# A two-layer decoder on one NeuronCore: the fourth convolution tile ahead of the state-space scan moves from TensorE to ScalarE and VectorE

## The reference

```
xn = x * rsqrt(mean(x * x, -1) + EPS) * norm_w            # x is already layer-normalised
x_inner, z = split(einsum('bld,ed->ble', xn, in_proj_w))  # 512 channels each
xc = conv1d(x_inner, conv_w, causal, 4 taps, one filter per channel) + conv_b
xc = silu(xc)
x_ssm = einsum('bld,ed->ble', xc, x_proj_w)               # 16 B, 16 C, 1 dt for each token
dt = softplus(x_ssm[..., -1:] * dt_w[:, 0] + dt_b)        # 512 channels
h  = exp(dt * A) * h + (dt * xc) * B ;  y = sum(h * C) + D_param * xc      # the scan, 128 steps
out = (y * silu(z)) @ out_proj_w + x
```

## Time and profile before

| | |
|---|---|
| median of 3 runs | 904.55 us (903.81 to 906.38) |
| the profiled execution | 906.09 us, its span 904.3 us |
| busy: PE, PEld | 732.1 us (81%), 525.2 us (58%) |
| busy: DVE | 718.4 us (79%) |
| busy: ACT | 541.4 us (60%) |
| busy: POOL | 521.5 us (58%) |
| mean granted TensorE clock | 0.898 |

### The profile page before, as it was taken

One profiled execution on the slowest core, in us unless ns is written; L12 is line 12 of the kernel. 1 busy time (PEld: TensorE's weight loads), 2 busy tenths in 40 slices (PEclk: granted clock), 3 DMA queues, 4 the chain that ended last, 5 costly groups with the idle time before them and its releaser, 6 DMA issues. The chain is left out here.

```text
span 904.3 us, 14551 instructions
## 1 busy us (share of the span) xinstructions
PE 732.1 (81%) x4298; PEld 525.2 (58%) x4301; DVE 718.4 (79%) x1533; ACT 541.4 (60%) x1377; POOL 521.5 (58%) x542
## 2 busy tenths in 40 slices
PE   5899999999999884499999149959999999940365
PEld 3578888888888762377777124345555555630232
DVE  6667788888898875677777578497999999679886
ACT  2545565555556552466666525778998788037195
POOL 2057777777777861355553576627888799422211
PEclk8899999999999997599999559969999999975586
DMA  8726000000000500365546230032223222100000
GB/s 315 226 85 289 1 2 1 8 1 7 8 1 8 200 7 12 122 226 147 147 143 124 75 100 29 4 117 70 93 93 100 87 94 93 37 10 0 0 18 30
DMA packets 29932, 70.80 MB, mean 78 GB/s; under 512 B 5440, under 2 KB 19584, under 8 KB 27552
## 3 DMA queue, kind: packets, MB, share of 16 engines
q1 hardware_dynamic: 25248, 57.28, 17.5%
q0 software_dynamic: 4608, 12.59, 5.6%
HBM read 59.30 MB, written 10.55 MB: 77 GB/s over the span
## 5 line engine op out<-in xcount | busy, mean ns | idle before, releaser
L1857 POOL TENSOR_TENSOR arena<-arena 128x1024 f32<-128x1024 f32 x63 | 148.4, 2382 | 45.7 <-DVE arena L1779 45.7
L1779 DVE TENSOR_TENSOR_SCAN arena<-arena,ps 128x1024 f32<-128x1024 f32 x64 | 143.7, 2277 | 12.6 <-PE ps L1504 7.3
L1525 PE MATMUL ps<-arena 128*128 128x512 f32 x256 | 120.1, 592 | 0.0
L645 PE MATMUL ps<-arena 128*128 128x128 f32 (+1 forms) x768 | 101.1, 282 | 0.9 <-PEq L373 0.9
L1086 POOL DMA_INDIRECT arena<-tokens,arena x64 | 62.6, 979 | 67.4 <-PE ps L1114 50.5
L645 PEld LDWEIGHTS ps<-arena 128*128 128x128 f32 (+1 forms) x768 | 91.6, 193 | 14.1 <-issue 12.9
L850 ACT ACTIVATE arena<-arena 128x128 f32<-128x128 f32 x256 | 98.8, 389 | 1.2 <-DVE arena L774 1.1
L858 ACT ACTIVATE arena<-ps 128x512 f32<-128x512 f32 x64 | 38.2, 597 | 86.6 <-PE ps L664 86.6
L1652 ACT ACTIVATE arena<-arena 128x1016 f32<-128x1016 f32 x64 | 72.3, 1135 | 19.1 <-DVE arena L1779 19.1
L1667 ACT ACTIVATE arena<-arena 128x256 f32<-128x256 f32 x192 | 81.3, 494 | 0.1
L905 POOL TENSOR_TENSOR arena<-arena 128x512 f32<-128x512 f32 x64 | 66.6, 1041 | 22.3 <-DVE arena L780 22.3
(11 more groups left out here) (324 smaller groups left out, 1617.2 us busy)
## 6 DMA issues: line engine op xcount, KB each, us to landing
arena<-c_rows SPq DMA_DIRECT2D x32, 512.0 KB, 3.5
arena<-in_E_gu SPq DMA_DIRECT2D x8, 1024.0 KB, 13.4
expert_out<-arena SPq DMA_DIRECT2D x64, 128.0 KB, 2.4
arena<-in_E_dn SPq DMA_DIRECT2D x1, 4096.0 KB, 13.0
arena<-in_ctxT SPq DMA_DIRECT2D x2, 1024.0 KB, 5.9
arena<-in_A_o SPq DMA_DIRECT2D x1, 2048.0 KB, 16.6
arena<-in_X_o SPq DMA_DIRECT2D x1, 2048.0 KB, 22.7
arena<-in_F_w SPq DMA_DIRECT2D x2, 1024.0 KB, 6.9
```

The lines of the kernel that those rows point to most:

```text
L645: t = eng.matmul(ps[:, i % 2, j * P:(j + 1) * P], L["wq"][0:L["kc"], c, GH * g + j, :], src[0:L["kc"], c, b * P:(b + 1) * P], start=c == 0 ...
L1525: t = eng.matmul(ps[:, 2 * k + r, :], ident, half(hC[s % 4], r), start=False, stop=n == ST - 1)
L1779: eng.tensor_tensor_scan(hst[s % 4], dA[s % 4], psD[s % 2].rearrange("p k m -> p (k m)"), 0.0, ALU.mult, ALU.add).then_inc(h_ready, 1)
L1857: eng.tensor_tensor(hC[s % 4], hst[s % 4], Csb[i % 4], ALU.mult).then_inc(hC_ready, 1)
```

## The change

The convolution of the fourth tile is computed like the other three: ScalarE writes the last tap and the bias (a fourth Identity in each half), VectorE adds the three others. The diagonal weights (with the four ScalarE copies that built them, L1564), the two groups of diagonal matmuls and the order in which the tiles were taken for their sake go. ScalarE no longer computes |zz| (`magnitudes`); VectorE clears the sign bit of zz behind each of its affine instructions in `steps` (a new instruction, with a wait for the one ahead of it), and ScalarE's exponentials wait for the tiles one by one. On VectorE the convolutions of half 0 are spread: `conv(0, 0)` behind combine 5 instead of 4, `conv(1, 0)` between combines 6 and 7, `conv(2, 0)` and `conv(3, 0)` where `conv(1, 0)` and `conv(2, 0)` were. TensorE's waits for the padding and for the xi copies, which stood ahead of the diagonal matmuls, go with them.

```diff
@@ -1327,7 +1327,6 @@
         padded = [view(room[11] + 1048 * c, 1048, "p (b t) -> p b t", b=NB) for c in range(CT)]
-        diagW = view(room[8], 512, "p (k m) -> p k m", k=KCONV)
         bcf, bct = B_[9], B_[10].bitcast(bf16)[:, 0:1024]
@@ -1338,7 +1337,7 @@
         z_moved = sem("z_moved")
-        diag_in, diag_done = sem("diag_in"), sem("conv_diag_done")
+        diag_in = sem("diag_in")
         s_conv, conv_ready, xc_ready = sem("conv_step"), sem("conv_ready"), sem("xc_ready")
@@ -1352,8 +1351,7 @@
         Z_BANK = ((5, 6, 7, 4), (2, 3, 6, 4))
-        DIAG_BANK, PROJ_BANK = (0, 5), (4, 7)
-        XC_ORDER = ((0, 3, 1, 2), (0, 1, 2, 3))
+        PROJ_BANK = (4, 7)
 
@@ -1417,17 +1415,11 @@
 
-                def conv_diag(k):
-                    for j in range(KCONV):
-                        t = eng.matmul(ps[:, DIAG_BANK[k], :].rearrange(tq, b=HB), diagW[:, j],
-                                       padded[CT - 1][:, k * HB:(k + 1) * HB, j:j + P], start=j == 0, stop=j == KCONV - 1)
-                    t.then_inc(diag_done, 1)
-
                 def bc_dt(k):
-                    for n, c in enumerate(XC_ORDER[k]):
-                        eng.wait_ge(xc_ready, CT * k + n + 1)
+                    for c in range(CT):
+                        eng.wait_ge(xc_ready, CT * k + c + 1)
                         t = eng.matmul(ps[0:3 * E + 1, PROJ_BANK[k], :], w_bc[:, c, :], half(xc[:, c], k),
-                                       start=n == 0, stop=n == CT - 1)
+                                       start=c == 0, stop=c == CT - 1)
                     t.then_inc(proj_done, 1)
@@ -1452,11 +1444,6 @@
                     project(CT + m, Z_BANK[0][m], 0).then_inc(z_done, 1)
-                eng.wait_ge(diag_in, KCONV)
-                eng.wait_ge(pad_ready, CT)
-                eng.wait_ge(xi_ready, CT)
-                conv_diag(0)
-
                 eng.wait_ge(z_ready, CT)
@@ -1464,8 +1451,6 @@
                 dt_rows(0)
-                eng.wait_ge(xi_ready, 2 * CT)
-                conv_diag(1)
                 bc_dt(1)
@@ -1540,7 +1525,7 @@
                         turn_dtu(3)
-                        eng.wait_ge(diag_in, KCONV + CT)
+                        eng.wait_ge(diag_in, CT)
                     if s == SLOTS:
@@ -1559,46 +1544,30 @@
                 loaded(eng, "vecs")
-                w0 = KCONV * (CT - 1)
-                for j in range(KCONV):
-                    eng.activation(diagW[:, j], ident, ACT.Copy, scale=cw[:, w0 + j:w0 + j + 1]).then_inc(diag_in, 1)
                 for c in range(CT):
...
                     eng.wait_ge(xi_done, CT * k + n + 1)
-                    if m < CT - 1:
-                        last = KCONV * m + KCONV - 1
-                        eng.activation(half(xc[:, m], k), ps[:, XI_BANK[k][m], :], ACT.Identity, bias=cb[:, m:m + 1],
-                                       scale=cw[:, last:last + 1])
+                    last = KCONV * m + KCONV - 1
+                    eng.activation(half(xc[:, m], k), ps[:, XI_BANK[k][m], :], ACT.Identity, bias=cb[:, m:m + 1],
+                                   scale=cw[:, last:last + 1])
                     eng.activation(padded[m][:, k * HB:(k + 1) * HB, PAD:], ps[:, XI_BANK[k][m], :].rearrange(tq, b=HB),
...
                 def conv_silu(n, k):
-                    c = XC_ORDER[k][n]
-                    if c < CT - 1:
-                        eng.wait_ge(conv_ready, (CT - 1) * k + c + 1)
-                        eng.activation(half(xc[:, c], k), half(xc[:, c], k), ACT.Silu).then_inc(xc_ready, 1)
-                    else:
-                        eng.wait_ge(diag_done, k + 1)
-                        eng.activation(half(xc[:, c], k), ps[:, DIAG_BANK[k], :], ACT.Silu,
-                                       bias=cb[:, c:c + 1]).then_inc(xc_ready, 1)
+                    eng.wait_ge(conv_ready, CT * k + n + 1)
+                    eng.activation(half(xc[:, n], k), half(xc[:, n], k), ACT.Silu).then_inc(xc_ready, 1)
 
...
 
-                def magnitudes(k):
-                    eng.wait_ge(dt_done, k + 1)
+                def exponentials(k):
                     for c in range(CT):
-                        eng.activation(half(dtu[:, c], k), ps[:, k, :], ACT.Abs, bias=dtb[:, c:c + 1],
-                                       scale=dtw[:, c:c + 1]).then_inc(abs_ready, 1)
-
-                def exponentials(k):
-                    eng.wait_ge(abs_ready, CT * (k + 1))
-                    for c in range(CT):
+                        eng.wait_ge(abs_ready, CT * k + c + 1)
                         eng.activation(half(dtu[:, c], k), half(dtu[:, c], k), ACT.Exp, scale=-1.0).then_inc(exp_ready, 1)
@@ -1622,13 +1591,11 @@
                 bc_rows(0)
-                magnitudes(0)
                 conv_silu(2, 1)
...
                 bc_rows(1)
-                magnitudes(1)
                 exponentials(1)
@@ -1711,10 +1678,13 @@
                 def steps(k):
-                    eng.wait_ge(abs_ready, CT * (k + 1))
+                    eng.wait_ge(dt_done, k + 1)
                     for c in range(CT):
...
                                           dtb[:, c:c + 1], ALU.mult, ALU.add).then_inc(zz_ready, 1)
+                        eng.wait_ge(zz_ready, CT * k + c + 1)
+                        eng.tensor_scalar(half(dtu[:, c], k).bitcast(u32), half(dts[:, c], k).bitcast(u32), 0x7FFFFFFF, None,
+                                          ALU.bitwise_and).then_inc(abs_ready, 1)
 
@@ -1743,15 +1713,17 @@
                 combine(HB)
+                combine(HB + 1)
                 conv(0, 0)
-                for b in range(HB + 1, NB):
-                    combine(b)
+                combine(HB + 2)
+                conv(1, 0)
+                combine(HB + 3)
                 normS.dve_variance(eng, 1)
                 scales_in(eng, cs, 1)
-                conv(1, 0)
+                conv(2, 0)
                 scales_out(eng, cs, 1)
-                conv(2, 0)
-                for c in range(CT - 1):
+                conv(3, 0)
+                for c in range(CT):
                     conv(c, 1)
```

## The result

The changed kernel takes 907.43 us (median of 20 runs, 902.28 to 911.41) where the kernel before takes 903.79 (20 runs, 900.82 to 909.0). The ratio is 1.0034, with a 95% interval of 1.0018 to 1.0049: slower by 3.1 us (1.6 to 4.4). The forecast was slower by 1.4, as 905.95; the time lies inside its range and above its likeliest value, and the difference is over twice the forecast one.

A forecast was written before the change was run, and what follows sets the result against it. Bound by ScalarE's copies, the dt matmul and z projections, not VectorE. Clock 2.06 and fourth convolution 2.14 put VectorE on the path; copy +0.57, dt matmul +0.78: 1.4 us later, added to median 904.55 gives 905.95; range 902.2 to 908.6.

The forecast's parts named there:

- What bounds the kernel, and the scan's fixed length: Ahead of the scan: ScalarE's copy, dt matmul and z projections set its start; delays reach the end, scan length unchanged.
- Combines and convolutions interleaved at no cost: VectorE, half 0: spread convolutions fill waits, the last combine ends as before, the fourth tile (2.33 us) costs nothing.
- The first pause lowers the clock, 2.06 us: TensorE idles 4.0 us ahead of the half-1 transposes; the clock falls, and ScalarE's first pass comes 2.06 us later.
- The rival in which the clock holds: TensorE's first pause leaves the clock up, so the 2.06 us goes away: 903.9 us, chance 0.17.
- Twelve convolution instructions in 9.8 us: VectorE, half 1: twelve instead of nine instructions take 9.8 us (9.3 to 10.2) instead of 7.66, adding 2.14.
- the collision in the sign clearing: Rival: VectorE's half-0 sign clearings wait out GpSimd's split, 1.31 us each: 909.2 us, chance 0.20 shared with a late clock.
- Sign clearing 0.50 each: VectorE, behind each of four affine instructions per half: 0.50 us each, so half-0 steps take 2.97+4·0.50 us.
- To the copy, +0.57: ScalarE's copy of the half-1 rows, behind the half-0 Exps, comes at 578.2 instead of 577.65.
- Dt matmul +0.78, z projections 0: TensorE after its second pause: low clock adds 0.78 us to the dt matmul; z projections lose 1.70 again, as before.
- Hidden work behind it: VectorE's half-1 steps, ScalarE's Exps and first Ln end a microsecond ahead of the step tile, costing nothing.
- The two times named as signs: If right: ScalarE's copy of the half-1 rows near 578.2 and VectorE's first step tile near 590.5.
- the upper end of the forecast's case: With the clock falling (chance 0.52), unknown ends of convolutions, sign clearing and dt matmul give 904.4 to 907.6 us.

The follow-up runs named there:

- the kernel with three edits: Changed kernel with the half-1 row copy ahead of the half-0 Exps, TensorE's first pause filled and VectorE's negation of A behind the half-1 steps: ratio 0.9968.
- the one with four: The kernel with three edits, with GpSimd's first split also held until VectorE's last convolution: ratio 0.996, 900.3 us.
- the second pair of profiles: Kernel before and changed kernel each run and profiled once more, without edits: 903.97 us and 907.91 us.

## Why the prediction was right, point by point

**What bounds the kernel, and the scan's fixed length: right.** The path ran through ScalarE's copy, the dt matmul and the z projections, and what came later there reached the end. (The prediction speaks once of eight z projections; its row has 16 matmuls, for four tiles, as it says further on.) Scan and tail took 308.9 us before and 308.6 after.

**Combines and convolutions interleaved at no cost: right.** The half-0 order came out as written, and the order alone holds the ratio at 1. The convolution at 538.65 had its cover, and the last combine came 18.01 us into the stretch (548.00), for 18.00 before.

**The first pause lowers the clock, 2.06 us: right,** with 2.31 measured (0.51 of the forecast 0.50 up to the projections, the rest inside them). The pause was 2.6 us and not the 4.0 forecast: the transposes came when they had (23.2 us into the stretch, 23.1 before), but the half-0 projections ended 1.7 us later, since the clock had come back later in them, as the windows show. It fell nevertheless. Filling the pause brings the first pass 1.6 to 1.9 us forward. The rival in which the clock holds is out in all five profiles that left this pause open: the first pass is at 29.83 to 30.78, never near 27.5. This clock is the main cause of the loss: with the pause filled the ratio is 1.0004, and with both filled 0.9999, though VectorE has all of its new work.

**Twelve convolution instructions in 9.8 us: this term was mis-sized,** and it is what failed. With the split behind them they took 9.45, 9.51 and 10.08 in three kernels. Beside it they took 10.07 to 11.40 in six profiles, 10.92 and 10.15 of them in the two of the changed kernel; four of the six lie above the forecast's upper end of 10.2. The forecast set the collision in the sign clearing, as a rival; it fell on the convolutions ahead of it. That rival had the right mechanism in the wrong place: the last two convolution instructions lose 1.12 us to the split in the profile after (1.09 and 1.53 for 0.75 each), and 1.04 from the kernel with three edits to the one with four. The Trainium skill ("SBUF — State Buffer", section "SBUF: two separate sides") says that VectorE and GpSimd take the shared ports as an exclusive lock for a whole instruction, where VectorE's is in a two-port mode or has two inputs in SBUF and GpSimd's reads SBUF. The prediction took up only the first of these two kinds; the convolution, with two inputs in the arena, is the second. The 1.53 us convolution beside a 1.47 us subtraction agrees with the rule, as does 0.43 for each half-0 sign clearing once GpSimd is held.

**Sign clearing 0.50 each: right,** with 0.43 to 0.66 in half 0, a mean of 0.52; the half-0 steps took 5.15 (forecast 4.97). The point from which the rival decides, a mean of 0.83, was not reached.

**To the copy, +0.57: +2.06 measured.** This is the sum of the above: 0.25 of the clock, 1.12 of the convolutions and 0.18 of the steps make 1.55, against the 1.49 missed.

**Dt matmul +0.78, z projections 0: right** in size (0.95 and 0.08 in the profiled pair). The z projections are the least certain term, for they come out at 7.13 or at 8.83 in the kernel before, without any edit. Forecast and measurement happened to meet at the same level, and this is luck: in the second pair of profiles the dt matmul added nothing (1.12 both times) and the z projections 1.68 (7.13 and 8.81).

**Hidden work behind it: right.** VectorE's half-1 steps, the last Exps and the first Ln were done ahead of the step tile at 590.35.

The sum was thus short by 1.7 in the profiled pair: 1.5 at the copy and 0.17+0.08 on TensorE. Against the ratio it is short by the same 1.7, and this was enough to carry the result over the 0.3%: of its three outcomes the prediction gave this one, slower than 907.26, a chance of 0.22, and no real difference 0.66.

**Luck in the numbers.** The time is closer to the forecast (907.43 for 905.95) than the difference is, because the forecast was added to the median of three runs, 904.55, which is 0.76 above that of twenty. The two times named as signs, the copy near 578.2 and the step tile near 590.5, were met (577.83 and 590.35) only because the stretch began 1.88 us earlier in this profile; from its start both are late, by 1.5 and 1.7. And the upper end of the forecast's case is added up wrongly: 905.95 and 0.4, 1.1 and 0.3 make 907.75, not 907.6.

## What to carry to other kernels

When work is taken from an engine, ask what its pause does to the next work there. Here TensorE lost 3.6 us of a diagonal product, and the projections behind it became 2 us slower. When work is given to VectorE, look at which of GpSimd's instructions will lie beside it, for the longest row there and not only for the instruction that is new. A gain on one engine can stay hidden behind an in-order queue: here the freed TensorE time was worth 3 us only once ScalarE's copy no longer stood behind the Exps.

## What the runs showed of the hardware

**VectorE and GpSimd slow each other even in short instructions.** A convolution instruction takes 0.75 us where GpSimd stands still, up to 1.08 beside its updates of the residual rows and up to 1.53 beside the split; in two profiles updates took 2.27 us in place of 1.23. Twelve convolution instructions took from 9.45 to 11.40 us in nine profiles with the same code for them; a sign clearing 0.43 to 1.24. The 3.27 us row of the kernel before is there again after, at 603.60.

**The clock ahead of the z projections is not fixed by the program.** The kernel before gave 8.83 and 7.13 us for the same 16 matmuls with the same 1.47 us pause; the others gave 7.13 to 10.21. In four profiles (the first of the kernel before among them) it fell only as the projections began, with the dt matmul, which uses a single row of the array, between them and the pause. What decides stays open.

**ScalarE sometimes stands still in half 0.** The gap of 4.36 us ahead of its row at 548.50 names no engine, while the xi result that it reads was there near 544.6, by an estimate from the row ahead (542.88) and the 1.72 us from tile to tile at the full level:

```profile
548.50 0.78 ACT L1554 ACTIVATE arena<-ps,arena 128x512 f32<-128x512 f32 x1 [4.36 <-remote]
```

Gaps of this kind, 3.7 to 7 us, are in 13 of 14 profiles, and not in the first one of the kernel before. In four profiles they held the transposes back, so that TensorE's pause was 3.9 to 5.4 us and the first pass near 30 or 30.8. The cause was not tried.

**The start of the stretch scatters** from 525.0 to 531.9 us between profiles with the same code ahead of it. Why wasn't tried; it is why the stretch was measured from its own start.
